# One set of call orders, step distances and PSUM banks of a software-pipelined audio-tower kernel replaced by another

## Chip, cores and metric

The kernel runs on one core of one Trainium2 chip. The metric is the device time of one execution in microseconds (us). TensorE (PE) multiplies, VectorE (DVE), ScalarE (ACT) and GpSimd (POOL) compute, and SyncE (SP) does nothing here but issue all transfers.

## What is computed

```python
h = einsum('bnf,ef->bne', patches, W) + b              # 128 clips, 46 tokens, 90 channels x 16, D = 192
h = h + causal_attention(layernorm(h), Wq, Wk, Wv)      # one head of 192
x = layernorm(h)
logits = x @ W_gate.T + b_gate                          # 8 experts, top 2 of the softmax
qkv = x @ W_qkv.T + b_qkv + 2 * sum_n dispatch_n * (x @ A_n.T) @ B_n.T      # rank 16
h = h + softmax(q @ k.T / 4) @ v @ W_proj.T + b_proj    # 12 heads of 16
```

## The kernel before

The 128 clips are worked in 16 groups (g = 0 to 15) of 8 clips, that is 368 tokens, or 4 pairs of 92. Numbers are split in a high and a low f16 part, and three products stand for one product in f32, so nearly each result is copied twice: high by ACT, low by DVE or POOL.

A group passes through the following calls; n in brackets is the part of it.

- SP `load_next(half)`: raw clips into `raw`, 1035 KB a half (L497). ACT `high(0..7)` and POOL `low(0..15)` (L703) split them into `xs` and `xe`; `extra_rows` (L556) moves `xe` to other rows of `xs`. A load waits for the lows of the group before that read the same half: half 0 for low 7, half 1 for low 15. `extra_rows` waits for low 9.
- PE `tok(0..11)` (L1386 to L1388 on `ps_tok`), DVE `h_tile`, `stats1`, POOL `ln1`, ACT `xn_tile`, PE `xt`, `g_`, `v_`, `sc`, `pt` (L1530), `av`, DVE `h2_`, `stats2`, POOL `ln2` and `xn2_` (L744), PE `yt`, `ga_`: embedding, first attention, second normalisation. SP `h_to_pairs` (L571) moves h. `tok(0)` waits for `extra_rows` of its group to have landed.
- DVE `logits`, `ranks`, `dispatch`, POOL `ad_` (L711), PE `at` (L1577), ACT `ad_high`, DVE `ad_low`, PE `qk_(0..2)` and `cv(0..1)`: router, low-rank part, q, k and v.
- SP `qk_to_scratch` (L582) writes q and k to device memory, `stack_qk` (L595, L596) waits until that has landed and reads them back head by head, `place_v2` (L608) moves v.
- For each pair p: PE `s_(p)` (L1627), DVE `max2`, `shift`, ACT `exp2`, PE `p_(p)` (L1640), ACT and DVE `p2t`, PE `pv(p)`, DVE `norm2`. Then PE `ot`, `pr`, DVE `fin(0..1)` (L1319) into `h2b`, SP `store` (L616). POOL `h2b_` (L761) of group g, which fills the buffer that `fin` adds to, waits until `store` of group g-2 has landed. It stands in POOL's list behind `ad_` of group g+1.

Each engine has a list of calls in a fixed order, and walks through it 37 times (`STEPS`). In step s a call works on the group g for which `step_of(op, n, g) == s`: g + `LAG[op][n]` in general, moved by `MOVED[op][n]` for the first three and the last three groups. So the lists and distances fix, ahead of time, the order of all work on each engine. There is no clock and no barrier between steps: engines meet only at semaphores, and a call that waits holds up all that stands behind it on its engine. The step numbers of two engines need not agree.

`weights(0..4)` are calls that run only once, in the start: they transpose, split and scale weights on PE, ACT and DVE. On DVE `weights(3)` also holds `biases()` (L1069 to L1075), and `weights(4)` holds `value_bias()` and `clear_rooms()` (L1085 to L1087). `late_weights` on SP issues 6 loads.

PE writes its products into eight PSUM banks. Three of them (`ps_r`) are shared by 27 calls: `RING_AT` gives each its bank, and its order is that of PE's list. `bank_free` makes a call wait until DVE or ACT has read out what the last user of the bank wrote. `FREED` says who that is: `g0` after `pr1`, for instance, waits for `fin(1)`.

All transfers that SP issues share one hardware queue.

Of the kernel before, what the change touches and what calls it, by code (L numbers as in the profile page):

```python
# [56 lines left out]
LAG = {"extra_rows": (8,), "load_next": (6, 7), "h_to_pairs": (9,), "qk_to_scratch": (11,), "stack_qk": (11,),  # L57
    "place_v2": (11,), "lateload": (7,), "store": (13,), "low": (7, 7, 7, 7, 7, 7, 7, 7, 7, 7, 8, 8, 8, 8, 8, 8),
    "ad": (11,), "ln1": (9, 9, 9), "h2b": (12,), "ln2": (10,), "xn2": (10,), "xn2_twin": (10,), "g_high": (11, 12),
    "router_exp": (13,), "high": (9, 9, 9, 9, 9, 9, 10, 10), "wact": (7, 10, 11, 12, 13), "v_copy": (12, 12),  # L60
    "p2t_high": (14, 14, 15, 15), "exp1": (12,), "exp2": (14, 14, 14, 15), "ad_high": (13,), "p1t": (12,),
    "qk_high": (13, 13, 13), "xn_tile": (11, 11, 11), "o2_twin": (15,), "cv_high": (13, 13), "o_high": (15, 15),
    "xn_twin": (11,), "xn_high": (11, 11), "x2_high": (12, 12), "ga_copy": (12,), "norm2": (13, 13, 13, 14),
    "shift": (12, 13, 13, 13), "qk_low": (11, 12, 12), "stats2": (11,), "p2t_low": (13, 13, 13, 13),
    "cv_low": (12, 12), "wdve": (6, 7, 7, 8, 10), "o_low": (14, 14), "max2": (12, 12, 13, 13), "h_tile": (9, 9, 9),
    "xn_low": (10, 10), "stats1": (9, 9, 9), "x2_low": (11, 11), "fin": (14, 14), "g_low": (10, 10), "logits": (11,),
# [4 lines left out]


MOVED = {"extra_rows": ((6, 3, 0, 0, 0, 0),), "load_next": ((6, 4, 3, 0, 0, 0), (4, 3, 2, 0, 0, 0)),
    "h_to_pairs": ((4, 0, 0, 0, 1, 1),), "qk_to_scratch": ((0, 0, 0, 0, 0, 2),), "stack_qk": ((0, 0, 0, 0, 0, 2),),
    "place_v2": ((0, 0, 0, 0, 2, 5),), "store": ((0, 0, 0, 6, 6, 6),),
    "low": ((6, 5, 5, 0, 0, 0), (6, 5, 5, 0, 0, 0), (6, 5, 5, 0, 0, 0), (6, 5, 5, 0, 0, 0), (6, 5, 5, 0, 0, 0), (6, 5, 5, 0, 0, 0), (6, 5, 5, 0, 0, 0), (6, 5, 5, 0, 0, 0), (6, 5, 5, 0, 0, 0), (6, 5, 4, 0, 0, 0), (6, 5, 4, 0, 0, 0), (6, 5, 3, 0, 0, 0), (6, 5, 3, 0, 0, 0), (6, 5, 3, 0, 0, 0), (6, 5, 1, 0, 0, 0), (6, 5, 0, 0, 0, 0)),
# [3 lines left out]
    "high": ((6, 5, 3, 0, 0, 0), (6, 5, 3, 0, 0, 0), (6, 5, 2, 0, 0, 0), (5, 5, 1, 0, 0, 0), (5, 5, 1, 0, 0, 0), (5, 5, 1, 0, 0, 0), (5, 4, 1, 0, 0, 0), (5, 4, 1, 0, 0, 0)),  # L80
    "p2t_high": ((0, 0, 0, 0, 2, 3), (0, 0, 0, 0, 3, 3), (0, 0, 0, 0, 3, 3), (0, 0, 0, 0, 3, 4)),
    "exp2": ((0, 0, 0, 0, 0, 3), (0, 0, 0, 0, 2, 3), (0, 0, 0, 0, 3, 3), (0, 0, 0, 0, 3, 4)),
    "qk_high": ((0, 0, 0, 0, 0, 0), (0, 0, 0, 0, 0, 2), (0, 0, 0, 0, 0, 2)),
    "xn_tile": ((4, 0, 0, 0, 0, 0), (4, 0, 0, 0, 0, 0), (4, 0, 0, 0, 0, 0)), "o2_twin": ((0, 0, 0, 1, 3, 4),),
    "cv_high": ((0, 0, 0, 0, 0, 2), (0, 0, 0, 0, 0, 2)), "o_high": ((0, 0, 0, 2, 3, 5), (0, 0, 0, 3, 3, 6)),
    "xn_twin": ((3, 0, 0, 0, 0, 0),), "xn_high": ((2, 0, 0, 0, 0, 0), (2, 0, 0, 0, 0, 0)),
    "norm2": ((0, 0, 0, 0, 2, 4), (0, 0, 0, 0, 2, 5), (0, 0, 0, 0, 2, 6), (0, 0, 0, 0, 3, 6)),
    "shift": ((0, 0, 0, 0, 0, 3), (0, 0, 0, 0, 0, 3), (0, 0, 0, 0, 2, 4), (0, 0, 0, 0, 2, 4)),
    "qk_low": ((1, 0, 0, 0, 0, 0), (0, 0, 0, 0, 0, 0), (0, 0, 0, 0, 0, 0)), "stats2": ((3, 1, 0, 0, 0, 0),),
    "p2t_low": ((0, 0, 0, 0, 1, 3), (0, 0, 0, 0, 2, 4), (0, 0, 0, 0, 2, 4), (0, 0, 0, 0, 3, 5)),  # L90
    "cv_low": ((0, 0, 0, 0, 0, 2), (0, 0, 0, 0, 0, 2)), "o_low": ((0, 0, 0, 2, 3, 6), (0, 0, 0, 2, 4, 6)),
    "max2": ((0, 0, 0, 0, 0, 3), (0, 0, 0, 0, 0, 3), (0, 0, 0, 0, 2, 4), (0, 0, 0, 0, 2, 4)),
    "h_tile": ((4, 3, 3, 0, 0, 0), (4, 3, 2, 0, 0, 0), (4, 3, 1, 0, 0, 0)),
# [1688 lines left out]
```

## Time and profile before

| | us |
|---|---|
| median of 3 runs | 641.6 |
| lowest and highest run | 638.78, 643.91 |
| profiled execution | 648.41 |
| its span in the profile | 646.7 |
| PE busy in it | 588.4 |
| mean granted PE clock | 0.943 of 2.4 GHz |

The profile is one execution. Its page sums busy time by engine and instruction group; a trace behind it gives each instruction's start, duration and what ended the idle time before it. Times in the trace are us from the start of the span.

### The profile page before, as it was taken

What the parts mean: (1) busy time and instruction counts of PE and PEld (TensorE: products, weight loads), DVE (VectorE), ACT (ScalarE), POOL (GpSimd) and SP (SyncE); (2) the same over time, 40 slices, a digit from 0 to 9 for tenths busy, and PEclk for the clock granted to TensorE, in tenths of its full rate; (3) what the DMA queues carried; (4) which work ended last, traced back from release to release, by engine and by line L of the source; (5) the groups of instructions that cost most, each with busy time, mean ns of one, the idle gap of its engine ahead of it and who ended that gap; (6) DMA issues with size and microseconds to landing.
All of it is one profiled execution on the core that took longest, in us unless ns stands there. A gap on an engine that the chain in (4) does not pass through costs nothing.

```text
span 646.7 us, 20566 instructions
## 1 busy us (share of the span) xinstructions
PE 588.4 (91%) x7811; PEld 524.8 (81%) x7811; DVE 489.3 (76%) x1307; ACT 356.2 (55%) x688; POOL 384.8 (60%) x651
## 2 busy tenths in 40 slices
PE   3768888979999999999999999999999999897784
PEld 3647776959898989999999889898989898785684
DVE  5314476647988888888888888887888889997774
ACT  3447434636666666666666566656566545543431
POOL 7795956676767676676849394857676614321010
PEclk9978777979999999999999999999999999997957
DMA  8786743686686858586685949585868261624601
GB/s 207 163 190 95 177 99 85 101 192 126 135 151 147 161 137 157 129 170 137 156 155 134 177 120 177 120 159 127 155 141 159 55 103 42 107 59 74 122 5 35
DMA packets 60132, 83.15 MB, mean 129 GB/s; under 512 B 11754, under 2 KB 44087, under 8 KB 58499
## 3 DMA queue, kind: packets, MB, share of 16 engines
q1 hardware_dynamic: 60035, 81.85, 61.7%
q8 instruction: 62, 1.02, 0.8%
q14 instruction: 35, 0.29, 0.2%
HBM read 50.24 MB, written 13.57 MB: 99 GB/s over the span
## 4 chain that ended last, share of the span: by engine, by line
PE 52%; DMA 16%; SPq 10%; POOL 7%; DVE 7%; issue 5%; ACT 3%; POOLq 0%; DVEq 0%; ACTq 0%
PE ps_r L1394 16%; DMA out<-h2b 7%; POOL xs L703 5%; PE ps_tok L1386 4%; PE ps_p L1640 4%; PE ps_tok L1387 4%; PE ps_tok L1388 4%; PE ps_r L1386 3%; DMA qk_scratch<-qk 3%; SPq L571 3%; PE ps_s L1627 3%; PE ps_r L1388 3%; PE ps_r L1387 3%; SPq L608 2%; PE ps_r L1541 2%
## 5 line engine op out<-in xcount | busy, mean ns | idle before, releaser
L703 POOL TENSOR_TENSOR xs<-raw,xs 90x368 f16<-90x368 f32 x192 | 164.7, 886 | 11.6 <-ACT xs L797 11.6
L1386 PE MATMUL ps_tok<-w_tok,xs 128*128 128x192 f16 x576 | 145.6, 253 | 12.7 <-issue 7.9
L1387 PE MATMUL ps_tok<-w_tok,xs 128*128 128x192 f16 x576 | 144.9, 252 | 0.0
L1388 PE MATMUL ps_tok<-w_tok,xs 128*128 128x192 f16 x576 | 144.8, 251 | 0.0
L1386 PEld LDWEIGHTS ps_tok<-w_tok,xs 128*128 128x128 f16 x576 | 66.4, 115 | 16.3 <-issue 8.8
L797 ACT ACTIVATE xs<-raw 90x736 f16<-90x736 f32 x96 | 75.9, 812 | 0.1
L703 POOL TENSOR_TENSOR xe<-raw,xe 90x368 f16<-90x368 f32 x64 | 55.2, 882 | 26.1 <-ACT xe L797 26.1
L797 ACT ACTIVATE p2T<-ps_p 128x552 f16<-128x552 f32 x64 | 40.3, 630 | 54.7 <-PE ps_r L1388 50.9
L1387 PEld LDWEIGHTS ps_tok<-w_tok,xs 128*128 128x128 f16 x576 | 66.5, 115 | 1.8 <-issue 0.3
L1388 PEld LDWEIGHTS ps_tok<-w_tok,xs 128*128 128x128 f16 x576 | 66.4, 115 | 0.3
L711 POOL TENSOR_TENSOR ad<-ga,disp 128x384 f32<-128x384 f32 x16 | 13.4, 840 | 79.2 <-DVE disp L1217 79.2
L761 POOL TENSOR_TENSOR h2b<-h,b_pr_bc 92x768 f32<-92x768 f32 x16 | 29.6, 1848 | 49.7 <-DMA out<-h2b 49.7
L1640 PE MATMUL ps_p<-ident,p 110*128 110x110 f32 x384 | 49.7, 268 | 4.0 <-DVE p2T L1135 3.2
L924 ACT ACTIVATE qk<-ps_r,b_qk 128x368 f16<-128x368 f32 x48 | 27.1, 565 | 47.4 <-PE ps_r L1388 47.4
L1394 PE MATMUL ps_r<-x2T,w_qk 128*128 128x368 f16 x240 | 48.8, 337 | 3.5 <-DVE adT L1108 3.2
L1386 PE MATMUL ps_r<-v,p2T 128*128 128x68 f16 x384 | 46.0, 201 | 4.3 <-DVE p2T L1135 2.8
L1119 DVE TENSOR_REDUCE mx<-ps_s 128x12 f32<-128x552 f32 x64 | 46.2, 722 | 4.5 <-PE ps_s L1627 4.5
L1150 DVE TENSOR_TENSOR o<-ps_r,rc 46x192 f32<-46x192 f32 x128 | 45.5, 355 | 4.2
L1135 DVE TENSOR_TENSOR p2T<-ps_p,p2T 128x552 f16<-128x552 f32 x64 | 46.2, 722 | 2.8 <-ACT p2T L797 1.7
L1640 PEld LDWEIGHTS ps_p<-ident,p 110*128 110x128 f32 x384 | 42.6, 147 | 6.7 <-issue 2.6
L1127 DVE TENSOR_TENSOR df<-ps_s,mx 128x552 f32<-128x552 f32 x64 | 46.6, 727 | 1.8 <-ACT p L852 0.6
L1387 PE MATMUL ps_r<-v,p2T 128*128 128x68 f16 x384 | 46.0, 199 | 0.9 <-issue 0.9
(179 smaller groups left out, 1614.5 us busy)
## 6 DMA issues: line engine op xcount, KB each, us to landing
raw<-x SPq DMA_DIRECT2D x32, 1035.0 KB, 8.1
qk_scratch<-qk SPq DMA_DIRECT2D x32, 276.0 KB, 3.1
q<-qk_scratch SPq DMA_DIRECT2D x48, 138.0 KB, 4.9
k<-qk_scratch SPq DMA_DIRECT2D x48, 138.0 KB, 5.5
xs<-xe SPq DMA_DIRECT2D x30, 184.0 KB
v<-v2s SPq DMA_DIRECT2D x64, 76.5 KB, 7.8
out<-h2b SPq DMA_DIRECT2D x16, 240.0 KB
xs<-xe SPq DMA_DIRECT2D x15, 149.5 KB
```

Of the source, the lines that this page charges most:

```text
L703: nc.gpsimd.tensor_tensor(lo, src, hi, ALU.subtract).then_inc(s_lo, 1)
L761: nc.gpsimd.tensor_tensor(h2b[:, g % 2, :, :], h2[:, g % 2, :, :], b_pr_bc[:].unsqueeze(1).to_broadcast([PT_, PAIRS, D]), ALU.add).then_in ...
L797: return nc.scalar.activation(out_, in_, ACT.Copy, scale=scale)
L1119: nc.vector.tensor_reduce(mx[:].rearrange("p (a h) -> p a h", a=2), scores2(), AX_X, ALU.max).then_inc(s_mx, 1)
L1127: nc.vector.tensor_tensor(df[:].rearrange("p (a h) k -> p a h k", a=2), scores2(), mx[:].rearrange("p (a h) -> p a h", a=2).unsqueeze(3).t ...
L1135: nc.vector.tensor_tensor(p2T_used(1), ps_p_used(), p2T_used(0), ALU.subtract).then_inc(s_p2T, 1)
L1150: nc.vector.tensor_tensor(o2[r, p, 0:D].rearrange("p (h e) -> p h e", h=HEADS), pv[r, b, :, 0:HD], rc[r, p, :].unsqueeze(2).to_broadcast([ ...
L1386: mm(dst, stat[0], mov[0], start=start, stop=False)
L1387: mm(dst, stat[0], mov[1], start=False, stop=False)
L1388: return mm(dst, stat[1], mov[0], start=False, stop=stop)
L1394: last = mm(dst, stat(a), mov(b), start=start and n == 0, stop=stop and n == 4)
L1640: last = nc.tensor.transpose(ps_p[:, half, 128 * a:128 * a + ROWS], p2[0:ROWS, 6 * half + 2 * a:6 * half + 2 * a + 2, :].rearrange("p a b ...
```

## The change

No instruction is added or taken away. All five lists of calls, `LAG`, `MOVED` and `RING_AT` are replaced. `STEPS` stays 37. What follows are the new lists, cut to the parts that matter here, and the whole of SP's.

```diff
-LAG = {"extra_rows": (8,), "load_next": (6, 7), "h_to_pairs": (9,), "qk_to_scratch": (11,), "stack_qk": (11,),
...
+LAG = {"load_next": (6, 6), "h_to_pairs": (8,), "lateload": (6,), "qk_to_scratch": (10,), "place_v2": (10,),
+    "stack_qk": (10,), "store": (12,), "extra_rows": (6,), "low": (8, 8, 8, 8, 9, 9, 9, 9, 9, 9, 9, 9, 9, 9, 9, 9),
...
-    "p": (14, 14, 14, 15), "av": (12, 12), "qk": (13, 13, 13), "wpe": (6, 7, 8, 10, 12),
+    "wpe": (8, 8, 9, 10, 11), "p": (14, 14, 14, 14), "qk": (13, 13, 13), "cv": (13, 13),
...
-RING_AT = {"v0": 0, "sc": 2, "v1": 1, "pv1": 0, "at": 0, "pt": 1, "pv2": 2, "av0": 1, "qk0": 0, "av1": 2, "pv3": 1,
...
+RING_AT = {"qk0": 2, "qk1": 0, "cv0": 1, "qk2": 0, "cv1": 2, "ot0": 1, "ot1": 0, "pv0": 2, "xt0": 1, "pr0": 0,
+           "xt1": 2, "yt0": 1, "yt1": 0, "pr1": 2, "pv1": 1, "g0": 2, "ga": 0, "g1": 1, "v0": 2, "sc": 1, "pv2": 0,
+           "v1": 2, "pt": 1, "at": 0, "av0": 2, "av1": 0, "pv3": 1}
@@ sync
+                load_next(0)
+                h_to_pairs()
+                load_next(1)
+                late_weights()
+                qk_to_scratch()
+                place_v2()
+                stack_qk()
+                store()
                 extra_rows()
-                load_next(1)
-                h_to_pairs()
-                qk_to_scratch()
-                stack_qk()
-                load_next(0)
-                place_v2()
-                late_weights()
-                store()
@@ gpsimd
...
+                ln1(0)
+                low(10)
+                ad_()
+                h2b_()
...
+                low(0)
+                low(1)
+                ln2()
+                xn2_()
...
@@ vector
...
+                shift(3)
+                fin(1)
+                x2_low(1)
...
+                logits()
+                g_low(1)
+                ranks()
+                dispatch()
+                weights(3)
+                max1()
...
@@ tensor
...
+                pr(1)
+                tok(7)
+                pv(1)
+                g_(0)
+                ga_()
...
+                pt()
+                at()
+                tok(0)
+                av(0)
...
```

Written out with the groups, SP's order in a step of the middle is as follows (G is the group of `qk_to_scratch`).

- Before: qk_to_scratch G, stack_qk G, load_next(0) G+5, place_v2 G, store G-2, extra_rows G+4, load_next(1) G+5, h_to_pairs G+3.
- After: qk_to_scratch G, place_v2 G, stack_qk G, store G-2, extra_rows G+4, load_next(0) G+5, h_to_pairs G+3, load_next(1) G+5.

In the start, the order of some calls on PE is as follows (call and part, then the group behind the point).

- Before: weights(1), tok 0.1 to 3.1, xt 0.0, 1.0, tok 4.1 to 6.1, g 0.0, tok 7.1, v 0.0, g 1.0, weights(2), ... sc 0.0, ... pt 0.0, tok 11.1, av 0.0, 1.0, tok 0.2, weights(3), tok 1.2 ... yt 0.0, 1.0, ... ga 0.0 ... weights(4), ... at 0.0, ... qk 0.0.
- After: weights(1), weights(2), tok 0.1 to 3.1, xt 0.0, ... g 0.0, weights(3), g 1.0, ... sc 0.0, ... pt 0.0, tok 0.2, av 0.0, 1.0, tok 1.2 to 3.2, weights(4), xt 0.1, ... yt 0.0, 1.0, ... ga 0.0, ... at 0.0, tok 0.3, av 0.1, 1.1, qk 0.0.

In the end, SP's order is: before, qk_to_scratch 15, stack_qk 15, place_v2 15, store 13, 14, 15; after, qk_to_scratch 15, stack_qk 15, store 13, place_v2 15, store 14, 15.

## Rows read from the trace of the kernel before

**Rows 1.** The page: span, and PE's busy time with share and instructions.
```profile
span 646.7 us, 20566 instructions
PE 588.4 (91%) x7811; PEld 524.8 (81%) x7811; DVE 489.3 (76%) x1307; ACT 356.2 (55%) x688; POOL 384.8 (60%) x651
```

**Rows 2.** By stretches: busy us per engine, granted PE clock, DMA share, GB/s.
```profile
166.00:199.30 33.30, 33.30 (x483) 30.54 (x481) 28.56 (x80) 21.24 (x41) 23.42 (x40) 1.00 0.75 149
199.30:232.50 33.20, 33.20 (x481) 30.44 (x480) 28.54 (x80) 21.24 (x41) 23.38 (x40) 1.00 0.75 157
...
100.00:150.00 50.00, 42.51 (x414) 34.69 (x413) 29.67 (x88) 23.54 (x45) 30.75 (x55) 0.86 0.63 131
...
550.00:600.00 50.00, 43.09 (x611) 35.67 (x609) 43.85 (x110) 22.43 (x47) 11.92 (x20) 0.93 0.43 78
600.00:647.00 47.00, 32.52 (x450) 29.48 (x448) 29.27 (x60) 13.87 (x26) 1.84 (x1) 0.72 0.29 56
```

**Rows 3.** Timeline of PE: start of `pt` of groups 3, 8 and 13.
```profile
168.22 0.48 PE L1530 MATMUL ps_r<-ident,p 92*92 92x92 f32 x4
...
334.54 0.48 PE L1530 MATMUL ps_r<-ident,p 92*92 92x92 f32 x4
...
503.75 0.48 PE L1530 MATMUL ps_r<-ident,p 92*92 92x92 f32 x4
```

**Rows 4.** Timeline of POOL: two of 16 `h2b_`, idle time before them in brackets.
```profile
301.46 1.86 POOL L761 TENSOR_TENSOR h2b<-h,b_pr_bc 92x768 f32<-92x768 f32 x1 [1.62 <-DMA out<-h2b]
...
439.58 1.83 POOL L761 TENSOR_TENSOR h2b<-h,b_pr_bc 92x768 f32<-92x768 f32 x1 [4.95 <-DMA out<-h2b]
```

**Rows 5.** Timeline of SP in one step: start and duration of issuing.
```profile
322.29 0.43 SPq L497 DMA_DIRECT2D raw<-x  x1
322.81 2.67 SPq L608 DMA_DIRECT2D v<-v2s  x4
325.52 1.08 SPq L616 DMA_DIRECT2D out<-h2b  x2
326.71 2.18 SPq L556 DMA_DIRECT2D xs<-xe  x3
```

**Rows 6.** The chain that ended last: a store and an `extra_rows`, issue to landing.
```profile
326.16 10.20 DMA out<-h2b
...
127.93 11.82 DMA xs<-xe
```

**Rows 7.** The page, DMA issues: count, KB each, median us to landing.
```profile
raw<-x SPq DMA_DIRECT2D x32, 1035.0 KB, 8.1
qk_scratch<-qk SPq DMA_DIRECT2D x32, 276.0 KB, 3.1
```

**Rows 8.** Timeline of PE in the start: four waits, idle time in brackets.
```profile
50.97 0.32 PE L1386 MATMUL ps_tok<-w_tok,xs 128*128 128x192 f16 x1 [3.90 <-issue]
...
88.81 1.86 PE L1394 MATMUL ps_r<-w_ga,x2T 128*128 128x136 f16 x15 [3.21 <-DVE x2T L1108]
...
105.72 1.69 PE L1394 MATMUL ps_r<-x2T,w_qk 128*128 128x368 f16 x5 [3.21 <-DVE adT L1108]
...
139.84 0.33 PE L1386 MATMUL ps_tok<-w_tok,xs 128*128 128x192 f16 x1 [3.99 <-issue]
```

**Rows 9.** Timeline of DVE in the start: first and last of `biases`, then `clear_rooms`.
```profile
82.70 1.22 DVE L1069 TENSOR_SCALAR b_dim<-b_row 1x384 f32<-1x384 f32 x1
...
85.49 1.70 DVE L1075 SCALAR_TENSOR_TENSOR o2T<-b_v,o2T 128x92 f16<-128x92 f32 x2
...
102.33 2.78 DVE L1086 MEMSET v<- 128x3264 f32 x1 [0.63 <-issue]
```

**Rows 10.** Timeline of DVE: a `fin` of the middle.
```profile
223.26 0.55 DVE L1319 SCALAR_TENSOR_TENSOR h2b<-ps_r,h2b 92x384 f32<-92x384 f32 x1
```

**Rows 11.** Timelines near the end: last q and k of group 15, then its `s_(0)`.
```profile
600.43 0.60 DVE L1284 SCALAR_TENSOR_TENSOR qk<-ps_r,b_qk,qk 128x368 f16<-128x368 f32 x1 [0.27 <-ACT qk L924]
...
615.10 0.84 PE L1627 MATMUL ps_s<-k,q 48*64 48x46 f16 x24
```

More of the change, by code:

```diff
@@ L54 @@
 LOWS = [(half, blk, part) for half, blk in HIGHS for part in range(2)]
-LAG = {"extra_rows": (8,), "load_next": (6, 7), "h_to_pairs": (9,), "qk_to_scratch": (11,), "stack_qk": (11,),
[L58 to L66, printed above, removed]
[4 rows of a table removed]
@@ L73 @@
[L73 to L76, printed above, removed]
[3 rows of a table removed]
[L80 to L93, printed above, removed]
-    "xn_low": ((3, 3, 0, 0, 0, 0), (3, 3, 0, 0, 0, 0)),
-    "stats1": ((4, 3, 3, 0, 0, 0), (4, 3, 2, 0, 0, 0), (4, 3, 1, 0, 0, 0)),
-    "x2_low": ((2, 0, 0, 0, 0, 0), (2, 0, 0, 0, 0, 0)), "fin": ((0, 0, 0, 2, 4, 6), (0, 0, 0, 2, 5, 6)),
-    "g_low": ((3, 2, 0, 0, 0, 0), (3, 2, 0, 0, 0, 0)), "logits": ((2, 0, 0, 0, 0, 0),),
-    "ranks": ((2, 0, 0, 0, 0, 0),), "dispatch": ((2, 0, 0, 0, 0, 0),), "max1": ((3, 2, 0, 0, 0, 0),),
[3 rows of a table removed]
-    "tok": ((6, 4, 2, 0, 0, 0), (5, 4, 2, 0, 0, 0), (5, 4, 2, 0, 0, 0), (5, 4, 2, 0, 0, 0), (5, 4, 1, 0, 0, 0), (5, 4, 1, 0, 0, 0), (5, 4, 1, 0, 0, 0), (5, 4, 1, 0, 0, 0), (5, 2, 1, 0, 0, 0), (5, 2, 0, 0, 0, 0), (5, 2, 0, 0, 0, 0), (5, 2, 0, 0, 0, 0)),
[9 rows of a table removed]
@@ L990, in xn_high @@
                         copy(xnT[:, g % 2, 2 * kh, :], bank(f"xt{kh}")[:, 0:TG]).then_inc(s_xnh, 1)
+                xn_high(0)
+                exp2(2)
+                weights(0)
+                xn_high(1)
+                x2_high(0)
+                x2_high(1)
+                high(3)
+                high(4)
+                p2t(2)
+                weights(1)
+                exp2(3)
+                g_high(0)
+                weights(3)
+                ga_copy()
                 g_high(1)
@@ L1030, in step @@
-                weights(3)
-                p2t(1)
-                x2_high(0)
-                x2_high(1)
-                high(4)
-                exp2(2)
-                g_high(0)
-                high(5)
-                ga_copy()
+                p1t()
+                ad_high()
+                exp2(0)
+                xn_tile(0)
+                qk_high(0)
+                xn_tile(1)
+                qk_high(1)
+                high(0)
+                cv_high(0)
+                p2t(0)
@@ L1040, in _ @@
+                weights(4)
+                high(1)
+                o2_twin()
+                qk_high(2)
+                exp2(1)
+                cv_high(1)
+                xn_tile(2)
+                weights(2)
+                o_high(0)
+                high(2)
+                o_high(1)
+                xn_twin()
+                p2t(1)
             for s in range(STEPS):
@@ L1358, in step @@
                 dispatch()
+                weights(3)
                 max1()
[L1360 to L1362 removed]
+                norm2(2)
                 max2(0)
+                h_tile(2)
                 shift(0)
+                p2t(3)
                 ad_low()
[L1366 to L1367 removed]
                 stats1(2)
                 h2_(0)
[L1370 to L1374 removed]
+                h2_(1)
+                weights(1)
+                norm2(3)
+                max2(1)
+                shift(1)
+                qk_low(0)
+                qk_low(1)
+                stats2()
+                weights(4)
+                cv_low(0)
+                p2t(0)
+                qk_low(2)
+                max2(2)
+                cv_low(1)
+                shift(2)
+                o_low(0)
+                h_tile(0)
+                o_low(1)
+                norm2(0)
+                p2t(1)
+                xn_low(0)
+                fin(0)
             for s in range(STEPS):
```

200 lines of the change are left out of this document (84 added, 116 removed), and 37 rows, old and new, of tables (LAG, MOVED).

## Prediction

> **What bounds the kernel now.** I read the page first: PE is busy for 588.4 of 646.7 us [rows 1], so 58 us are left to be won by an order of calls, unless PE's own work gets cheaper. The busy time by stretches then says where they lie. In the full steps PE is never idle, its clock is whole, and DVE is busy 28.5 us, ACT 21.2, POOL 23.4 of some 33.3 [rows 2]. The starts of `pt`, one a group, give the period: (334.54 - 168.22) / 5 = 33.26 us, and 169.21 us instead of 166.3 for the next five groups [rows 3]. So there are three kinds of loss. Start: at 168.22 PE has reached the `pt` of group 3. Middle: 2.9 us between groups 8 and 13. End: in the last 97 us PE is busy 75.6 us at clocks of 0.93 and 0.72 [rows 2].
>
> The middle loss has a loop for its cause, and the POOL timeline shows it. `h2b_` waits 1.62 us for the landing of a store at group 9's step and 4.95 us four steps later [rows 4]. SP's timeline shows why: store is issued at 325.52, right behind a `raw` load of 1035 KB and the four v transfers, and `extra_rows` comes 1.2 us later [rows 5]. The store's second half lands 10.2 us after its issue [rows 6], where the small scratch writes take 3.1 us at the median [rows 7]. A late `h2b_` delays the lows behind it in POOL's list, these delay the next loads, and so the next store.
>
> In the start PE's timeline has four waits that matter, 3.90, 3.21, 3.21 and 3.99 us, 14.3 in all [rows 8]. The second comes behind `biases` on DVE, which run from 82.70 to 87.2 ahead of `x2_low` of group 0. The third comes behind `clear_rooms`, whose longest memset alone is 2.78 us, ahead of `ad_low` of group 0 [rows 9]. The fourth is `tok(0)` of group 4, waiting for `extra_rows`, issued behind a `raw` load and v, which took 11.82 us to land [rows 6].
>
> **The change, part by part.** To place calls I lay them in the new order and give each the distance from its start to the next start which it has in the full step of [rows 2]; all positions below are estimates from that, on PE, in us from the start of a new step.
>
> *Full steps.* The instructions are the same, so the floor of 33.26 us stays; the question is whether a wait shows. For the store: `pr(1)` of G-2 ends at 18.1, `fin(1)` takes 0.55 [rows 10], so SP issues at 19 with only `stack_qk` (issued about 12 to 15) ahead in the queue, and no raw load. I take 3 to 4 us to land, near the scratch write's 3.1; the bounds are 3.1 and 10.2 [rows 6, 7]. So it is there at 23, at worst at 29. POOL wants it after `ad_`, at about 26.5. So the wait of up to 4.95 us goes, and with it the loop. `extra_rows` waits for low 9, which waits for high 4, about 21.3; it is issued by 23.5 and wanted by `tok(0)` at 29.9. The 11.82 us of [rows 6] would miss that by 5; but that one had a raw load and v ahead of it, and here the raw load comes behind. Load 0 follows at 23.5, lands 8.1 later [rows 7], at 32, and is wanted by `high(0)` at 35.6. POOL and ACT, laid out the same way, are in time. The banks have less room: before, the closest pair of users is 1.75 us apart, after, `g_(0)` starts 1.3 us behind `pr(1)` and `av(0)` 1.4 us behind `v_(1)`. `fin(1)` needs 0.55 of the 1.3, and DVE must be free for it. My layout of DVE's list leaves 0.4 to 1 us at the four closest places. Middle, then: -2.9 us; bounds 0 (the store waits on) and -2.9.
>
> Here the Trainium skill bears on the store ("DMA: Bandwidth & Descriptors", "Queues, rings and completion order"): within an engine's ring descriptors are taken in order, but completion is not first in, first out, so a small transfer need not wait for all of a large one ahead. By that alone moving the load would bring less; the 10.2 us of [rows 6] against 3.1 of [rows 7] say that in this kernel it is nearly all of it.
>
> *Start, up to `qk_(0)` of group 0.* Three things move against it. `weights(1)` stands ahead of `high(5..7)` of group 1 on ACT, so lows 10 to 15 and the load behind them come some 8 us later; `late_weights` and `extra_rows` of group 2 follow them on SP, 2 us later than before. `high(4)` of group 2 now stands ahead of `g_high(0)` of group 0 and waits for that load, 2.5 us. And `tok(0)` of group 2 stands ahead of `av(0)` of group 0: its `extra_rows` land at about 74.6, so `av(0)` starts at 76, by my layout some 6 us later than now. For it: `weights(2)` falls in the 3.90 us in which PE waited anyway [rows 8]. `biases` run beside this wait for `tok(0)`, not ahead of `x2_low`; `clear_rooms` run before `ga_`, not ahead of `ad_low`. That takes out both 3.21 us waits [rows 8] and DVE's 4.5 and 2.8 us [rows 9] from the chain of group 0. Walking the chain: `ga_` of group 0 at 90.6 (88.81 before), `at` at 99.6, `qk_(0)` at 102 instead of 105.72, with 1.4 us more of PE's work behind it. That is -5 us. Bounds: +6 (`av(0)` late and nothing given back), -8 (nothing late).
>
> *Start, from `qk_(0)` to the full steps.* Before, 62.5 us pass to 168.22 for some 51.6 us of work; the rest is the 3.99 us wait and clock: 0.86 on average from 100 to 150 [rows 2]. In the new order `extra_rows` of group 4 has no raw load ahead of it; I place its landing at 128 to 129, and `tok(0)` at 128. That is 1 us of wait, so -3, and -1 us for the clock that this idle cost. Bounds 0 and -5.
>
> *End.* Both orders leave some 70 us of PE's work behind the last `tok`. q and k of group 15 come 2.4 us of work later; from the last of them to its first `s_` 14.7 us pass now [rows 11], transfers that neither order can hide. After that nearly as much work is left in both (12.1 and 12.7 us). `store` 13 now stands ahead of `place_v2` 15; `fin` of group 13 is done some 9 us before `pv(0)` of 15, which covers the transfers. The new order is denser at the very end. I take +1.5, bounds -1 and +4.
>
> **Sum.** Against the profiled execution: 646.7 - 2.9 - 5 - 4 + 1.5 = 636.3 us of span, with 1.7 outside it 638.0. The profiled execution is 6.8 above the median of the runs (648.41, 641.6), so 631.2; I say 631. With all bounds at their ends it would be 624.7 and 651.6.
>
> **The rivals.**
>
> *The start gives nothing* (no change). `av(0)` behind `tok(0)` and `g_high(0)` behind `high(4)` eat what the moved weights give. Then 641.6 - 2.9 + 1.5 = 640, or 638 with the wait for `extra_rows` gone in part. For it: the walk has some 60 links, and the late `av(0)` is plain in the lists. Against it: two 3.21 us waits have a cause that is moved away for sure. Chance 0.25.
>
> *DVE becomes the bound* (the other side). The banks' closest pairs go from 1.75 to 1.3 us and DVE is busy 28.5 of 33.3 us [rows 2]. If `fin(1)`, `norm2(1)` or `p1t` come late by more than the 0.4 to 1 us of room, PE waits in every step. Each us is worth 12 of them: 1.4 us a step gives 631 + 17 = 648, from where it is slower than now by over 1%; 2 us give 655. For it: the room is thin, in-order lists pass each delay on. Against: laid out from measured durations no call is late. Chance 0.12.
>
> *The store waits all the same* (the change does not do what it says). Landing stays at 10 us, `h2b_` waits 3 us or more, and the middle keeps its 2.9 us: 634. Chance 0.12, inside the range and still faster.
>
> *Steps get shorter than 33.26.* PE's weight loads are busy 30.5 of 33.3 us; if those were the floor, 14 full steps would give back up to 39 us, 592. In the rows PE is busy all through at whole clock and the period is the same to 0.01 us, so I give it 0.02. The Trainium skill says so in general ("Perfetto Trace Analysis", "Identifying the Most-Contended Engine"): matmul busy share does not measure headroom, weight-load share is to be read instead.
>
> **Chances.** Forecast, around 631 (623 to 636): 0.49. Store waits: 0.12. No gain in the start: 0.25. DVE bound: 0.12. Shorter steps: 0.02. About 1% is what a measurement of this kernel tells from no change, that is 635.2 to 648. Faster: 0.49 and 0.12 and 0.02, less the 0.02 of these cases that end above 635.2: 0.61. Slower: 0.12. Same: 0.27. The range leaves out the shorter steps and most of the DVE case: 621 to 646, its lower end the 624.7 of the bounds less some 3 us, as the lowest run lies under the median (638.78, 641.6).
>
> **What would show it.** Right: `pt` starts 33.26 us apart from group 3 to 13; no wait of `h2b_` for `out` in the middle; store landing within 5 us; `qk_(0)` of group 0 at about 102 us and `pt` of group 3 near 158; no wait over 2 us of PE at `tok(0)` of group 4; from `pt` of group 13 to the end 143 to 146 us, as now (646.7 - 503.75 = 143 [rows 1, 3]). Wrong: a wait of PE that returns in every step, at `g_(0)`, `av(0)` or `tok(0)`; `pt` of group 3 at 168 or later; `raw` landing after ACT wants it.

## The result, and the profile after

The changed kernel takes 634.52 us at the median of 4 runs (631.28 to 635.83), the kernel before 642.75 in the runs beside it (638.78 to 645.41). The ratio is 0.9879, with a 95% interval of 0.9833 to 0.9926. A second set of 4 runs gave 633.6 (ratio 0.9866, 0.981 to 0.9923). Here and below medians and ranges are those of all runs, and ratios leave out runs more than 1.5% above the fastest of their kernel, so that they differ by up to 0.002 from those of two medians. The change makes the kernel 1.2% faster, 8 us.

The page of the changed kernel. Beside [rows 1] the span is 12.9 us shorter, 10.7 of it idle time of PE (58.3 to 47.6) and 2.2 of it busy time.

```profile
span 633.8 us, 20566 instructions
PE 586.2 (92%) x7811; PEld 524.2 (83%) x7811; DVE 488.6 (77%) x1307; ACT 355.6 (56%) x688; POOL 386.4 (61%) x651
```

The timeline of PE at the starts of `pt` of groups 3, 8 and 13, as in [rows 3]; the lines of the changed kernel are those of before plus 4.

```profile
156.65 0.48 PE L1534 MATMUL ps_r<-ident,p 92*92 92x92 f32 x4
...
323.11 0.48 PE L1534 MATMUL ps_r<-ident,p 92*92 92x92 f32 x4
...
489.58 0.48 PE L1534 MATMUL ps_r<-ident,p 92*92 92x92 f32 x4
```

These three marks cut each kernel in start, middle and end. Before, they were 168.22, 335.53 and 142.95 us; now they are 156.65, 332.93 and 144.22. The start gave 11.6, the middle 2.6, and the end took 1.3, all read from one execution of each kernel.

The busy time by stretches, columns as in [rows 2]: one full step, the second five groups, the end.

```profile
156.65:189.94 33.29, 33.29 (x482) 30.42 (x480) 28.59 (x81) 21.14 (x42) 23.55 (x40) 1.00 0.72 159
323.11:489.58 166.47, 166.47 (x2397) 152.13 (x2396) 142.94 (x397) 105.72 (x206) 117.66 (x196) 1.00 0.67 145
489.58:633.80 144.22, 123.06 (x1687) 107.52 (x1685) 112.39 (x280) 58.95 (x121) 30.35 (x58) 0.87 0.33 65
```

PE is busy for all of the 166.47 us in which it was idle for 2.2 before. Of these 2.2 us some 1.3 were the loop's, and the timeline of POOL shows it gone, beside [rows 4]. Of the 16 `h2b_` only those of groups 14 and 15 wait, at the end of the kernel; from group 0 to 13 there is no wait in the list.

```profile
320.28 1.84 POOL L765 TENSOR_TENSOR h2b<-h,b_pr_bc 92x768 f32<-92x768 f32 x1
...
453.44 1.85 POOL L765 TENSOR_TENSOR h2b<-h,b_pr_bc 92x768 f32<-92x768 f32 x1
...
576.48 1.84 POOL L765 TENSOR_TENSOR h2b<-h,b_pr_bc 92x768 f32<-92x768 f32 x1 [1.32 <-DMA out<-h2b]
```

The timeline of SP in a step, beside [rows 5]: store and `extra_rows` go out ahead of the `raw` load, the store 0.03 us after `fin(1)` has ended (312.10 + 0.55).

```profile
312.68 0.82 SPq L620 DMA_DIRECT2D out<-h2b  x2
315.29 2.19 SPq L560 DMA_DIRECT2D xs<-xe  x3
317.52 0.54 SPq L501 DMA_DIRECT2D raw<-x  x1
```

The timeline of PE in the start: the waits over 0.5 us from 79 us on, beside [rows 8]. The first two are at `xt(0)` of group 1 and `yt(0)` of group 0, then come `qk_(0)` of group 0, `s_(0)` of group 0 and `tok(0)` of group 4. From there to 536.5 us PE waits once, for 0.29 us at 523.98.

```profile
79.00 0.55 PE L1482 MATMUL ps_r<-ident,xn 128*128 128x128 f32 x3 [2.62 <-ACT xn L978]
85.01 1.46 PE L1558 MATMUL ps_r<-ident,xn 92*128 92x92 f32 x8 [2.58 <-DVE xnT L1112]
101.61 0.94 PE L1398 MATMUL ps_r<-x2T,w_qk 128*128 128x368 f16 x5 [0.53 <-DVE h L1257]
123.43 0.56 PE L1631 MATMUL ps_s<-k,q 48*64 48x46 f16 x24 [1.14 <-DMA k<-qk_scratch]
127.04 0.25 PE L1390 MATMUL ps_tok<-w_tok,xs 128*128 128x192 f16 x1 [1.45 <-POOL xs L707]
```

### The profile page after: what moved, and what is told of

Its sections match the earlier page's. It is cut to its first block, busy times and chain, and to the rows that moved or that the text cites. A ratio compares the mean times of both kernels' runs of the same rounds, so it can differ in the third digit from the quotient of the medians.

```text
span 633.8 us, 20566 instructions
## 1 busy us (share of the span) xinstructions
PE 586.2 (92%) x7811; PEld 524.2 (83%) x7811; DVE 488.6 (77%) x1307; ACT 355.6 (56%) x688; POOL 386.4 (61%) x651
## 3 DMA queue, kind: packets, MB, share of 16 engines
q8 instruction: 62, 1.02, 0.8%
## 4 chain that ended last, share of the span: by engine, by line
PE 74%; DMA 7%; POOL 7%; DVE 4%; issue 3%; ACT 2%; SPq 2%; POOLq 0%; ACTq 0%; DVEq 0%
PE ps_r L1398 24%; PE ps_tok L1390 6%; PE ps_p L1644 6%; PE ps_tok L1392 6%; PE ps_tok L1391 6%; PE ps_s L1631 4%; POOL xs L707 4%; PE ps_r L1390 4%; PE ps_r L1392 4%; PE ps_r L1391 4%; PE ps_r L1545 3%; DMA raw<-x 2%; PE ps_r L1674 2%; DMA k<-qk_scratch 2%; PE ps_r L1558 1%
## 5 line engine op out<-in xcount | busy, mean ns | idle before, releaser
L707 POOL TENSOR_TENSOR xs<-raw,xs 90x368 f16<-90x368 f32 x192 | 166.4, 893 | 63.2 <-ACT xs L801 63.2
L1644 PE MATMUL ps_p<-ident,p 110*128 110x110 f32 x384 | 51.3, 273 | 3.0 <-DVE p2T L1139 3.0
L1390 PE MATMUL ps_r<-v,p2T 128*128 128x68 f16 x384 | 46.3, 201 | 4.5 <-DVE p2T L1139 3.7
L1398 PE MATMUL ps_r<-x2T,w_qk 128*128 128x368 f16 x240 | 46.0, 323 | 0.5 <-DVE h L1257 0.5
L1392 PE MATMUL ps_r<-v,p2T 128*128 128x68 f16 x384 | 46.3, 201 | 0.0
L1391 PE MATMUL ps_r<-v,p2T 128*128 128x68 f16 x384 | 46.3, 200 | 0.0
L685 POOL TENSOR_TENSOR rs<-ve,minus_half 128x1 f32<-128x1 f32 (+1 forms) x64 | 43.0, 672 | 5.0
```

Source lines behind the costliest of these rows:

```text
L685: nc.gpsimd.tensor_tensor(dst, ve, minus_half[0:rows, 0:cols], ALU.pow).then_inc(done, 1)
L707: nc.gpsimd.tensor_tensor(lo, src, hi, ALU.subtract).then_inc(s_lo, 1)
L1390: mm(dst, stat[0], mov[0], start=start, stop=False)
L1391: mm(dst, stat[0], mov[1], start=False, stop=False)
L1392: return mm(dst, stat[1], mov[0], start=False, stop=stop)
L1398: last = mm(dst, stat(a), mov(b), start=start and n == 0, stop=stop and n == 4)
```

## The experiments

The question is which part of the change brings the gain. For this each of the five lists was written out call by call with its group, for the old and the new kernel, so that a single call, or one engine's whole list, can be exchanged. The banks always belong to PE's list. Line numbers of PE in these kernels are 197 or 198 above those of before (L1386 is L1583 or L1584). This table holds all runs of the study. The three stretches are read from the starts of `pt` in the one profiled execution of each; median and ratio are those of the timed runs. They were taken in four sets, each beside runs of the kernel before (medians of 642.75, 642.42, 642.39 and 642.04). So kernels of different sets are compared by their ratios; where a difference in us is worked out from ratios, 1 stands for 642 us.

| kernel | median us (lowest, highest; runs) | ratio to before, 95% | start | middle | end |
|---|---|---|---|---|---|
| before, first profile | 641.6 (638.78, 643.91; 3) | 1 | 168.22 | 335.53 | 142.95 |
| before_again | 643.59 (638.38, 647.5; 10) | 1.0012, 0.9975 to 1.0048 | 164.84 | 336.31 | 142.45 |
| before_sp_new | 639.49 (635.69, 643.27; 10) | 0.9975, 0.9941 to 1.001 | 164.33 | 334.32 | 141.65 |
| before_weights_new | 643.07 (641.18, 646.28; 10) | 1.0007, 0.9967 to 1.0046 | 163.80 | 337.62 | 139.58 |
| before_both | 636.93 (634.05, 639.41; 10) | 0.9929, 0.9896 to 0.9963 | 161.29 | 334.05 | 141.66 |
| before_sp_act | 634.5 (633.88, 639.9; 5) | 0.9882, 0.982 to 0.9945 | 160.30 | 334.05 | 143.85 |
| before_three | 631.47 (630.36, 632.28; 4) | 0.9824, 0.9785 to 0.9863 | 156.83 | 332.63 | 140.64 |
| after | 634.52 (631.28, 635.83; 4) | 0.9879, 0.9833 to 0.9926 | 156.65 | 332.93 | 144.22 |
| after_again | 633.6 (632.04, 635.05; 4) | 0.9866, 0.981 to 0.9923 | 157.83 | 332.93 | 142.54 |
| after_two_back | 633.23 (631.75, 636.85; 4) | 0.9872, 0.9818 to 0.9925 | 154.11 | 332.93 | 142.96 |
| after_sp_old | 687.29 (680.94, 690.35; 4) | 1.0681, 1.0604 to 1.0759 | 173.59 | 363.10 | 142.51 |
| after_dve_15 | 661.1 (657.98, 661.94; 4) | 1.0278, 1.0231 to 1.0324 | 158.69 | 347.58 | 153.93 |
| after_end_old | 637.7 (635.58, 642.0; 10) | 0.9936, 0.9903 to 0.9969 | 155.75 | 340.03 | 142.12 |
| two_back_end_old | 640.23 (636.2, 645.37; 10) | 0.9967, 0.9922 to 1.0012 | 154.96 | 341.13 | 138.11 |

### The kernel before, a second time

No edit.

> The kernel before, once more, for a second profiled execution; the first one (648.41) lay 5.7 us above the median of its runs, and I subtracted that excess from the changed kernel too. Theory A (the excess lies in the middle loop of store, `h2b_` and load, which starts by chance and feeds itself): the times spread over 5 us or more, and a profile near 641 shows 166.3 to 167 us from `pt` of group 8 to that of 13 instead of 169.21, with waits of `h2b_` under 2 us. Rival B (the excess is in the start or the end, or in the clock): the ten groups from `pt` of 3 to 13 take 335.5 us again, and `pt` of group 3 or the end moves instead.

The start moved: `pt` of group 3 stands at 164.84 instead of 168.22. The middle took 336.31, not less than the 335.53 of the first profile, and `h2b_` waited up to 5.25 us again. So theory A fell: the middle loop is not a matter of chance. It is there in both profiled executions of this kernel, and what moved by 3.4 us is the start. That also gives a measure for all that follows: marks of single profiles that differ by less than 3 us in the start tell nothing alone.

### One list of the old kernel changed: SP's

```diff
@@ sync, all steps, kernel before
-qk_to_scratch G, stack_qk G, load_next(0) G+5, place_v2 G, store G-2, extra_rows G+4, load_next(1) G+5, h_to_pairs G+3
+qk_to_scratch G, place_v2 G, stack_qk G, store G-2, extra_rows G+4, load_next(0) G+5, h_to_pairs G+3, load_next(1) G+5
```

> The kernel before with one list changed: SP issues in the order of the changed kernel (store and extra_rows ahead of load_next(0), place_v2 ahead of stack_qk). Lists and distances of the other four engines and the banks stay. Theory (the order of transfers makes the middle loop and the 3.99 us wait for extra_rows of group 4): store lands in under 5 us, `h2b_` waits under 0.5 us in the middle, 332.6 us instead of 335.5 between `pt` of groups 3 and 13, and tok(0) of group 4 waits about 1 us; the whole 4 to 6 us shorter than before (ratio 0.991 to 0.994). Rival (the greater distance between fin, store and `h2b_` in the lists of POOL and DVE is what helps; SP's order alone does nothing): waits of `h2b_` of 3 us or more stay, ratio 0.998 to 1.002. A third outcome, slower than before by 1% or more, would say that load 0, now issued later, lands too late for the highs of the old lists.

The loop is gone: `h2b_` waits nowhere between groups 0 and 12. The ratio of 0.9975 is a gain of 1.6 us, which its interval doesn't separate from nothing. Two things took the rest. The wait of `tok(0)` of group 4 for `extra_rows` is no more, but there is another in its place. Timelines of ACT and of PE, 128 to 139 us:

```profile
135.24 0.82 ACT L994 ACTIVATE xe<-raw 90x736 f16<-90x736 f32 x1 [6.52 <-DMA raw<-x]
135.96 0.55 ACT L1121 ACTIVATE qk<-ps_r,b_qk 128x368 f16<-128x368 f32 x1
```

```profile
137.20 1.71 PE L1591 MATMUL ps_r<-x2T,w_qk 128*128 128x368 f16 x5 [4.16 <-DVE qk L1481]
...
367.01 0.19 PE L1584 MATMUL ps_r<-v,p2T 128*128 128x68 f16 x1 [1.52 <-issue]
```

The `raw` load is now the one that comes late. ACT waits 6.52 us for it at `high(0)` of group 5, and `qk_high(0)` stands behind that call; so PE waits 4.16 us for the bank, as long as it had waited before for `extra_rows` (3.99, [rows 8]). The third outcome that I had named as a possibility is there, at one place. The last row is a wait of PE in the middle that is not the loop's; it comes back below.

### Only the weights moved

```diff
@@ tensor, scalar and vector, start, kernel before
-PE: weights(2) behind g_(1).0; weights(3) behind tok(0).2; weights(4) behind sc.1
+PE: weights(2) behind weights(1); weights(3) behind g_(0).0; weights(4) behind tok(3).2
-DVE: weights(3) behind stats1(0).2, ahead of x2_low(0).0; weights(4) behind max1.1, ahead of ad_low.0
+DVE: weights(3) behind g_low(1).0; weights(4) behind h_tile(0).2
 ...
```

> The kernel before with only the calls weights(0..4) of PE, ACT and DVE moved to the neighbours that they have in the changed kernel (biases beside the wait for tok(0), clear_rooms ahead of the work on group 1's xn). Theory (these two stand in group 0's chain and their two waits of 3.21 us are the start's loss): qk_(0) of group 0 starts 5 to 6 us earlier than 105.72, at about 100, and pt of group 3 some 5 us earlier than 168.22 or as much as the wait of tok(0) of group 4 lets through; ratio 0.990 to 0.994. Rival 1 (the weights are hidden anyway, and the start's gain is from SP's order and from highs and toks standing elsewhere): qk_(0) at 104 or later, pt of group 3 at 167 to 169, ratio 0.998 to 1.002. Rival 2 (transfers bound the start: what comes earlier on PE waits longer at tok(0) of group 4): qk_(0) near 100, the wait of tok(0) of group 4 grows from 3.99 to about 9 us, pt of group 3 at 167 to 168.

By its time (a ratio of 1.0007) this edit does nothing. None of the three expectations fits the rows: `qk_(0)` came at 103.51, as in before_again (103.42), `pt` of group 3 at 163.80 beside 164.84 in before_again. Rival 2 is nearest, in that transfers are later. From `at` to `qk_(0)` of group 0 it now takes 2.2 us instead of 5.6, so the 3.21 us of `clear_rooms` are out of the chain. But `ga_` of group 0 starts at 94.60, 5 to 6 us later than before: weights(1) of ACT now stands ahead of highs of group 1, and the `raw` loads that wait for their lows go out at 45.55 and 53.37 instead of 40.42 and 46.36. PE's timeline has new waits ahead of `ga_`, and that for `extra_rows` of group 4 is 4.95 us (3.99 and 4.55 in the two executions of before).

```profile
55.74 0.32 PE L1584 MATMUL ps_tok<-w_tok,xs 128*128 128x192 f16 x1 [4.42 <-issue]
...
86.30 1.86 PE L1676 MATMUL ps_r<-ident,xn 128*128 128x128 f32 x6 [3.39 <-ACT xn L1172]
...
136.73 0.33 PE L1584 MATMUL ps_tok<-w_tok,xs 128*128 128x192 f16 x1 [4.95 <-issue]
```

### Both, then with three calls of ACT

> Both edits together in the kernel before: SP's new order and the new places of weights(0..4). Theory: the two add up, as they touch different stretches: pt of group 3 at about 160 (5 us from the weights, 3 from extra_rows of group 4), 332.6 us from there to pt of group 13, 143 us behind it, as before; the whole some 9 to 11 us shorter than before (ratio 0.983 to 0.987), that is all that the change gives. Rival: more than 3 us of the start's gain is missing (pt of group 3 later than 162), so the rest of the start's lists (highs, toks, lows) carries a part that I had booked as a cost.

The two edits are worth 4.6 us together (a ratio of 0.9929), where one gave 1.6 and the other nothing. But the Rival is near too: ACT still waits 6.22 us for `raw` at `high(0)` of group 5 and PE 3.87 us behind it. The third edit takes `qk_high` out from behind this load.

```diff
@@ scalar, groups 4 to 15, kernel before with both edits
-p1t, p2t(3), high(0) G+4, qk_high(0) G, xn_tile(0), high(1) G+4, high(2) G+4, exp2(0), qk_high(1) G, qk_high(2) G, ...
+p1t, p2t(3), qk_high(0) G, xn_tile(0), exp2(0), qk_high(1) G, high(0) G+4, qk_high(2) G, high(1) G+4, ..., cv_high(0) G, high(2) G+4
```

> The kernel before with three edits: SP's new order, the new places of weights(0..4), and in ACT's list high(0), high(1) and high(2) of a group moved behind qk_high(1), qk_high(2) and cv_high(0) of four groups back, where the changed kernel has them. With the first two edits alone ACT waited 6.22 us for the raw load at high(0) of group 5 with qk_high(0) behind it, and PE 3.87 us for that. Theory (this wait is what still lay between the two edits and the changed kernel): ACT's wait falls under 3 us or holds up nobody, PE's wait at 135 goes, `pt` of group 3 at 157 to 158.5, the middle 334, ratio to before 0.986 to 0.989. Rival (other calls of the start carry the rest, the toks of PE and lows of POOL): PE's wait moves to tok(0) of group 4 or 5, `pt` of group 3 later than 160, ratio 0.991 to 0.995.

The theory holds and more: 631.47 us, a ratio of 0.9824. No run of this kernel took as long as the shortest of before_both (634.05). In the timeline of ACT the `high(0)` no longer waits, and `qk_high(0)` and (1) stand ahead of it; in the busy time by stretches PE is never idle from group 3 to 13.

```profile
130.46 0.57 ACT L1122 ACTIVATE qk<-ps_r,b_qk 128x368 f16<-128x368 f32 x1 [3.56 <-PE ps_r L1586]
...
133.76 0.57 ACT L1122 ACTIVATE qk<-ps_r,b_qk 128x368 f16<-128x368 f32 x1 [1.74 <-PE ps_r L1586]
134.23 0.80 ACT L995 ACTIVATE xe<-raw 90x736 f16<-90x736 f32 x1
```

```profile
156.83:489.46 332.63, 332.63 (x4792) 304.97 (x4791) 285.34 (x791) 208.61 (x410) 235.05 (x391) 1.00 0.70 150
```

### The same without the weights

The edit is that of before_three without the moved weights.

> The kernel before with SP's new order and the three highs of ACT behind qk_high(1), qk_high(2) and cv_high(0), but with weights(0..4) where the kernel before has them; that is the kernel with three edits (631.47) without the edit of the weights. Theory of the prediction (biases and clear_rooms in group 0's chain cost 5 us): a wait of 3.2 us behind each of them, qk_(0) of group 0 at 101 to 103 instead of 99.87, `pt` of group 3 at 159.5 to 162, 634.5 to 637 us, ratio 0.987 to 0.991. Rival (the weights alone gave nothing, 643.07 to 642.42, and give nothing here: transfers set the start): `pt` of group 3 at 156.5 to 158, 631 to 632.5 us, ratio 0.981 to 0.984.

634.5 us is the edge of the first theory. The weights' new places are worth 3.7 us here (ratios of 0.9882 and 0.9824; their intervals overlap). The profiled execution of this kernel took 639.9 us, 5.4 above its median, so its three stretches are those of a long execution. The wait for `clear_rooms` is back in the timeline of PE, at the length that [rows 8] has:

```profile
101.10 0.94 PE L1592 MATMUL ps_r<-x2T,w_qk 128*128 128x368 f16 x5 [3.20 <-DVE adT L1306]
```

The ratios form a ladder. SP's order: 1 to 0.9975, -1.6 us. ACT's three highs on top: to 0.9882, -6.0; or with the weights in it, 0.9929 to 0.9824, -6.7, and of the steps from one edited kernel to the next only this one is clear of noise by its intervals (0.9896 to 0.9963 and 0.9785 to 0.9863). The weights: +0.4 alone, -3.0 with SP's order, -3.7 with SP's order and ACT's. Neither SP's order nor the weights alone is separated from nothing, all three edits give 11 us. ACT's three highs alone, in the kernel before, were not run.

### SP's old order in the new kernel

```diff
@@ sync, all steps, changed kernel
-qk_to_scratch G, place_v2 G, stack_qk G, store G-2, extra_rows G+4, load_next(0) G+5, h_to_pairs G+3, load_next(1) G+5
+qk_to_scratch G, stack_qk G, load_next(0) G+5, place_v2 G, store G-2, extra_rows G+4, load_next(1) G+5, h_to_pairs G+3
```

> The changed kernel with SP's list of the kernel before (load_next(0) ahead of place_v2, store and extra_rows); the other four lists and the banks stay new. Theory (SP's order makes the loop of store, `h2b_` and load): waits of `h2b_` for out of 1 us or more come back in the middle and the store lands 8 us or more after its issue; they reach PE only where the lists have no slack, so 333 to 335.5 us from `pt` of group 3 to that of 13; `pt` of group 3 later than 156.65 by 2 to 5 us, as extra_rows of group 4 goes behind a raw load again; ratio to before 0.991 to 0.997. Rival (the new lists of the four computing engines keep the distances that matter, and SP's order is of no account in them): `pt` of 3 at 156 to 157, 333 us from 3 to 13, ratio 0.985 to 0.990 like the changed kernel.

The Rival fell, and the theory had the mechanism and a price some ten times too small: 687.29 us, 53 more than the changed kernel. Timelines of SP, POOL and PE in one step:

```profile
232.22 0.42 SPq L793 DMA_DIRECT2D k<-qk_scratch  x1
238.19 0.35 SPq L694 DMA_DIRECT2D raw<-x  x1
...
241.70 1.10 SPq L813 DMA_DIRECT2D out<-h2b  x2
242.90 2.20 SPq L753 DMA_DIRECT2D xs<-xe  x3
```

```profile
236.42 1.75 POOL L900 TENSOR_TENSOR xs<-raw,xs 90x368 f16<-90x368 f32 x2 [3.85 <-ACT xs L994]
...
248.73 1.84 POOL L958 TENSOR_TENSOR h2b<-h,b_pr_bc 92x768 f32<-92x768 f32 x1 [3.84 <-DMA out<-h2b]
```

```profile
249.91 0.25 PE L1583 MATMUL ps_tok<-w_tok,xs 128*128 128x192 f16 x1 [1.42 <-issue]
```

SP stands from 232.6 to 238.19 at load_next(0), which waits for low 7 (POOL, ended 238.17). `fin(1)` was done at 237.21 and low 9 at 239.84; store and `extra_rows` go out at 241.70 and 242.90, behind this load and v. So the store is issued 4.5 us after its data was there: 1.0 of it is the wait for low 7, and in the rest SP issues the load and v, which it could not do while it stood. Then comes the landing: `h2b_` goes on at 248.73, 7.0 us after the store's issue. In the kernel before, the same order held up only the landing (store issued at 325.52, `fin(1)` done at 325.07). How much of the 53 us is late issue, how much slow landing, and how much the load or v, which both moved ahead of the store, no run separates. PE waits for `extra_rows` at `tok(0)` in nearly every step, 1.42 to 2.63 us, and everything behind is late by as much, the lows too. The steps are 34.9 to 36.1 us, or 38.3 to 38.9 where the clock falls as well; 36.3 on average over the ten groups, beside 33.29. Two stretches as long as such steps:

```profile
209.11:247.86 38.75, 36.67 (x482) 32.42 (x481) 28.80 (x80) 21.16 (x41) 23.59 (x39) 0.91 0.62 131
247.86:283.20 35.34, 33.92 (x486) 30.78 (x484) 29.06 (x81) 21.60 (x43) 23.59 (x39) 1.00 0.68 140
```

### The two calls that I had booked against the new start

```diff
@@ tensor, start, changed kernel
-pt.0, tok(0).2, av(0).0, av(1).0
+pt.0, av(0).0, av(1).0, tok(0).2
@@ scalar
-high(4).2, g_high(0).0
+g_high(0).0, high(4).2
```

> The changed kernel with the two calls put back that I had booked against it: tok(0) of group 2 behind av(0) and av(1) of group 0 on PE, and high(4) of group 2 behind g_high(0) of group 0 on ACT. Theory of the prediction (each holds up group 0's chain): av(0) of group 0 does not wait for the extra rows, `ga_` starts at 88 instead of 90.51, qk_(0) at 99 to 100 instead of 101.61, and `pt` of group 3 1 to 2 us earlier than 156.65 unless a load sets it; ratio to before 0.984 to 0.987. Rival (the start is set by transfers and by POOL from there on, group 0's chain has slack): qk_(0) earlier, `pt` of group 3 the same within 0.5 us, ratio 0.986 to 0.990.

`pt` of group 3 starts at 154.11, and at 154.96 in two_back_end_old, which has the same start, against 156.65, 157.83 and 155.75 in the three kernels without the edit: 2.2 us earlier on average. The time moved by 0.4 to 1.3 us (633.23 against 633.6 and 634.52), which is not separated from nothing.

### Room on DVE

```diff
 dve.wait_ge(p_pr, g * 2 + (n + 1))
+if n == 1:
+    nc.vector.memset(idle_room[:, 0:1800], 0.0)
 nc.vector.scalar_tensor_tensor(out=h2b[...], in0=bank("pr1")...)
```

> The changed kernel with one more instruction of DVE a group: a memset of 1800 f32 a partition into a tile that nobody reads, between the wait of fin(1) for pr(1) and fin(1) itself; at the 2.78 us of 3264 that is 1.53 us. DVE is then busy 30.1 of 33.3 us. Theory of the prediction (the banks leave 0.4 to 1 us for DVE at the closest places, and g_(0) follows pr(1) closely): PE waits 0.5 to 1.1 us a step for fin(1) or norm2(1), the period is 33.8 to 34.4 us, the whole 6 to 13 us longer than the changed kernel. Rival (pv(1) stands between pr(1) and g_(0), and DVE's 4.8 idle us a step take it up): period 33.3, the whole at most 2 us longer.

The memset takes 1.56 us, and at `g_(0)` PE waits 1.23 us for `fin(1)`, in every step. The starts of `pt` are 34.68 us apart, 1.39 more than 33.29. Timelines of DVE and of PE:

```profile
320.12 1.56 DVE L1326 MEMSET idle_room<- 128x1800 f32 x1 [0.99 <-PE ps_r L1402]
```

```profile
322.23 0.94 PE L1402 MATMUL ps_r<-xnT,w_m 128*128 128x368 f16 x5 [1.23 <-DVE h2b L1327]
```

So the room at this place is 1.56 - 1.23 = 0.33 us by the wait, or 0.17 us by the longer step. The kernel takes 27 us more than the changed one. The theory is right in the place, and the price was above its 6 to 13: the middle alone is 14.7 us longer (13.9 in the ten steps, the rest one more wait at 403.45), the end 10 to 11, where most of PE's waits are for DVE. DVE's idle time of 4.8 us a step doesn't help, it lies elsewhere in the step.

### The changed kernel again, and two with the old end

> The changed kernel once more, beside the other three of this set, for its own time on the same chip and a second profiled execution. Expected: ratio to before 0.985 to 0.990, `pt` of group 3 at 155 to 158, 332.9 us to `pt` of group 13, 143 to 144.5 us behind it. If `pt` of group 3 or the end moves by 2 us or more between two executions, differences of that size between single profiles of other kernels say nothing by themselves.

As expected, with 1.2 us of change in the start and 1.7 in the end between two executions of one kernel.

The lists of old and new have done exactly the same calls at one point near `at` of group 9. The next two kernels take the new lists up to there and the old ones behind.

> The changed kernel up to at of group 9 on PE and the calls beside it on the other engines, and from there the lists, distances and banks of the kernel before (both orders have done exactly the same calls at this point of PE's, DVE's, ACT's and POOL's lists). It isolates the end. Theory of the prediction (the new end costs 1.5 us, bounds -1 and +4): `pt` of group 3 as in the changed kernel, no wait of PE at the seam over 1 us, 332.8 us to `pt` of group 13, and 141 to 143 us from there to the end instead of 144.22; ratio to before 0.984 to 0.987. Rival (the two ends are worth the same, what differs is where `pt` stands in the list): 1 us or more is lost elsewhere, ratio 0.987 to 0.990.

> A kernel that should beat both: the changed kernel with tok(0) of group 2 behind av(0) and av(1) of group 0 and high(4) of group 2 behind g_high(0) of group 0 (`pt` of group 3 at 154.11 with these), and from at of group 9 the lists of the kernel before (140.64 us behind `pt` of 13 in the kernel with three edits). If the two add up: 154 to 155.5, 332.8 and 141 to 142.5 us, a span of 628 to 630.5 and a time of 629.5 to 632, ratio 0.980 to 0.984. Rival (single profiles differ by 2 us and more, the parts are not worth what they read): 632 to 634, ratio 0.984 to 0.988.

Both missed. The seam costs 7.1 and 8.2 us (middle of 340.03 and 341.13 instead of 332.93): for some steps the engines' lists don't fit each other, and PE waits twice for over 1 us (3.14 and 1.66), first for a late `qk_low`.

```profile
398.12 0.95 PE L1591 MATMUL ps_r<-x2T,w_qk 128*128 128x368 f16 x5 [3.14 <-DVE qk L1481]
```

The ends of 142.12 and 138.11 us say that the old lists are not worse there, but the times can't settle it behind such a seam. The kernel that I had built to beat both does not; before_three is the fastest one of the study.

## Why the prediction was right, and where its steps failed

The time, 634.5 us, is in the range and on the side that I gave most chance. The steps are less right than the sum, and part of its nearness is luck: terms that were off in opposite ways cancelled.

**Middle, -2.9.** The span gave 2.6. The loop is the cause of only part of it: with SP's order in the old kernel the loop is gone, and 1.5 us of PE's wait stay, at a `pv` call at 367.01, which the profile puts down to nothing it shows. In the first profile of before it is 0.92 us (at 370.34), and there the loop's own waits, for `p2T`, are the other 1.3. All profiles of kernels with PE's old list but that of before_three have this wait, at the same call; none of those with PE's new list has it there. The rest of the difference is the floor: a step is 33.29 us now and was 33.26, which is +0.3 over ten groups. My floor "stays" was off by this.

**Landing of the store, 3 to 4 us.** It can be read only where somebody waits for it, at the end: issued at 597.49, awaited until 601.76, so at most 4.3; the one before it, right behind six reads of q and k, issued at 569.41, awaited until 576.48, so 7. In the middle only "in time" is shown: issued at 312.68, landed by 320.28, when `h2b_` starts. So "within 5 us" is shown at one place and missed at another. And after_sp_old shows what I left out: a load ahead of the store in SP's list also holds back the store's issue, by 4.5 us with v's transfers.

**Start up to `qk_(0)`, -5.** 102 was predicted and 101.61 came; `ga_` 90.6 and 90.51, `at` 99.6 and 98.52. The second execution had 100.14, but that of the kernel before had 103.42 instead of 105.72, so some 2 us of either kernel's value are chance. But the terms were wrong in part. I had put `av(0)` of group 0 at 76, behind a late `extra_rows`; it started at 70.79 with no wait. The `raw` load was late as I had worked out (54.05 instead of 46.36), but `extra_rows` needs only low 9 and was issued at 64.73, as before (64.74). On the other side PE has two new waits of 2.6 us at `xt(0)` and `yt(0)`, in the rows at the top, which I did not have. The weights, which were to bring all of the 5, are worth 3.0 to 3.7, and nothing at all without SP's new order.

**From `qk_(0)` to the full steps, -4.** The marks give it: `pt` of group 3 stood near 158 in the text (168.22 - 5 - 4 is 159.2) and came at 156.65 and 157.83, against 168.22 and 164.84. The step that failed is its cause. I wrote that `extra_rows` with no raw load ahead of it ends the 3.99 us wait. It does, but by SP's order alone the load behind it is late, ACT waits for that, and PE waits 4.16 us at the next call. The edit that removes this, `high(0)` behind `qk_high(1)` in ACT's list, appears in my text only as a number that the walk produced ("wanted at 35.6"), never as a term; it is worth 6.0 to 6.7 us by the ratios, the largest of the three. In this kernel a part costed one by one came out at too little for ACT and too much for the weights, and the two errors cancelled.

**End, +1.5.** Nine profiles with the old lists at the end have 138.11 to 143.85 us behind `pt` of 13, mean 141.4; four with the new ones 142.51 to 144.22, mean 143.1 (the one with the longer DVE left out). That is +1.6, but it is a mean over single executions that differ by 1.7 us and more, and partly by what else was changed; the direct test failed at its seam.

**From profile to median, -6.8.** This was the largest error in the number: 638.0 - 6.8. The profiled execution of the changed kernel lay 1.3 us above its median, not 6.8. before_again shows that some 3 us of the first profile were in the start. An excess of one execution is not a constant that another kernel inherits. With it left at the 1.3 that came, the sum would have been 636.7, 2 us above the result instead of 3.5 below.

**The rivals.** Start gives nothing: fell, `pt` of group 3 is 7 to 11.6 us earlier, outside what executions differ by. DVE as the bound: did not come, but by 0.2 to 0.3 us; "0.4 to 1 us of room" was too kind, and a us of wait costs some 21 (26.6 / 1.23) and not the 12 that I counted, as the end pays too. The store waits all the same: fell, and its price of 2.9 us was wrong; with these lists a late SP costs 53 us. Shorter steps: fell, 33.29.

The three edits of before_three reach a ratio of 0.9824, some 3 us below the changed kernel (intervals 0.9785 to 0.9863 and 0.981 to 0.9923, which overlap). So what the change brings over before can be had by SP's order, ACT's three highs and the weights; the other moved calls and the new banks bring nothing more that was seen. Against it stand 0.3 us of the floor and perhaps the 1.6 of the end.

## What to carry to other kernels

When all transfers go through one queue issued by one engine, move its list together with the lists that consume what it brings: a wait removed at one consumer comes back at the next one. SP's order alone gave 1.6 us, inside the noise, and the weights alone nothing, all three edits 11. Read what stands behind each waiting call of the issuing engine: order in the queue and order of waits are two different costs. Before relying on a thin gap in a repeated step, put a known delay into it; what it gives in one run (0.2 to 0.3 us here) is better than a layout. And take two profiles of the kernel before, so that one execution's chance is not booked as a term.
